# Decoder layer on one core: attention scores with the keys stationary and the queries moving

## The reference, cut to what matters

```
x = x + rg_lru(layernorm(x))
ln = layernorm(layernorm(x)); xn = layernorm(ctx)
q = (ln @ Wq + bq) * 128**-0.5
k, v = split(concat([xn, ln], axis=1) @ Wkv + bkv)
out = softmax(q k^T) v                       # per batch and head: 100 x 822
x = x + (out merged over heads) @ Wo + bo
x = x + expert(argmax(route)) * max_prob     # per token
```

## Time and profile before

| | us |
|---|---|
| three runs of the kernel | 1041.38, 1042.39, 1042.47 |
| median of the runs | 1042.39 |
| span of the profiled execution, first to last instruction | 1041.8 |
| recurrent block and projections, up to the first score | 160.6 |
| the eight batches, first score to first product with Wv | 527.2 |
| Wv, Wo, router, experts | 354.0 |

### The profile page before, as it was taken

How to read it: one execution, slowest core, us unless ns; L and a number is a source line. 1 busy time by engine, 2 the same in 40 slices (tenths; PEclk the granted TensorE clock), 3 DMA queues, 4 the chain that set the end, 5 groups by cost and what they waited for, 6 DMA issues and landing times.

```text
span 1041.8 us, 18196 instructions
## 1 busy us (share of the span) xinstructions
PE 1019.0 (98%) x6086; PEld 934.4 (90%) x6087; DVE 811.0 (78%) x1392; ACT 561.8 (54%) x1111; POOL 115.4 (11%) x98
## 2 busy tenths in 40 slices
PE   8999999999999999999999999999999999999997
PEld 7969998999999999999999999998967788888886
DVE  7888666888979879798797996675858856947992
ACT  4425575445544455454554545573646756847871
POOL 3623200000000000000000000000011111211221
PEclk9999999999999999999999999999999999999999
DMA  8433884343323443234433335479367974956970
GB/s 273 128 116 128 308 300 164 91 172 121 112 93 96 170 119 109 98 96 154 131 95 116 96 93 178 145 253 323 108 189 258 340 259 154 358 184 223 363 270 22
DMA packets 110279, 182.47 MB, mean 175 GB/s; under 512 B 32464, under 2 KB 53456, under 8 KB 108322
## 3 DMA queue, kind: packets, MB, share of 16 engines
q1 hardware_dynamic: 108562, 177.45, 50.8%
q0 software_dynamic: 1680, 4.54, 1.3%
HBM read 145.84 MB, written 37.11 MB: 176 GB/s over the span
## 4 chain that ended last, share of the span: by engine, by line
PE 83%; DVE 7%; issue 3%; DMA 3%; ACT 2%; SPq 1%; ACTq 0%; POOL 0%; DVEq 0%; POOLq 0%
PE bank L641 24%; PE bank L643 24%; PE bank L642 24%; PE bank L1177 4%; PE bank L1316 1%; PE bank L1195 1%; PE bank L1164 1%; PE bank L1162 1%; PE bank L1194 1%; DMA w<-in_WoT 1%; DMA stage<-in_W 1%; DVE hs L1716 1%; SPq L686 1%; DVE xn_l L1645 1%; DMA scr_q<-st 1%
## 5 line engine op out<-in xcount | busy, mean ns | idle before, releaser
L641 PE MATMUL bank<-pt_h,xn_h 128*128 128x256 f32 (+1 forms) x576 | 167.4, 291 | 0.0
L643 PE MATMUL bank<-pt_h,xn_l 128*128 128x256 f32 (+1 forms) x576 | 164.8, 286 | 0.0
L642 PE MATMUL bank<-pt_l,xn_h 128*128 128x256 f32 (+1 forms) x576 | 164.7, 286 | 0.0
L1645 DVE TENSOR_TENSOR wsl<-stage,wsh 128x2048 fp32r<-128x2048 f32 x63 | 143.8, 2292 | 24.6 <-ACT wsh L1496 19.8
L641 PE MATMUL bank<-xt_h,qt_h 128*128 128x410 f32 (+1 forms) x384 | 136.4, 355 | 1.2 <-ACT pr L1451 1.2
L642 PE MATMUL bank<-xt_l,qt_h 128*128 128x410 f32 (+1 forms) x384 | 134.1, 349 | 0.0
L643 PE MATMUL bank<-xt_h,qt_l 128*128 128x410 f32 (+1 forms) x384 | 134.1, 349 | 0.0
L1496 ACT CAST wsh<-stage 128x2048 fp32r<-128x2048 f32 x63 | 120.5, 1920 | 12.6 <-PE bank L643 8.0
L641 PEld LDWEIGHTS bank<-pt_h,xn_h 128*128 128x128 f32 x576 | 109.0, 189 | 1.3 <-issue 0.2
L642 PEld LDWEIGHTS bank<-pt_l,xn_h 128*128 128x128 f32 x576 | 109.1, 189 | 0.0
L643 PEld LDWEIGHTS bank<-pt_h,xn_l 128*128 128x128 f32 x576 | 109.0, 189 | 0.0
(11 more groups left out here) (266 smaller groups left out, 2418.0 us busy)
## 6 DMA issues: line engine op xcount, KB each, us to landing
stage<-in_W SPq DMA_DIRECT2D x63, 1024.0 KB, 6.1
scr_q<-st SPq DMA_DIRECT2D x16, 800.0 KB, 4.2
qf<-scr_q SPq DMA_DIRECT2D x8, 1600.0 KB, 6.6
zr<-scr_z SPq DMA_DIRECT2D x16, 800.0 KB, 5.5
scr_z<-zf SPq DMA_DIRECT2D x7, 1600.0 KB, 5.2
rt<-in_ctxT SPq DMA_DIRECT2D x7, 1444.0 KB, 12.9
raw<-in_ctx SPq DMA_DIRECT2D x8, 768.0 KB, 4.6
mrow<-scr_rows SPq DMA_DIRECT2D x14, 361.0 KB, 3.9
```

The lines of the kernel that those rows point to most:

```text
L641: pe.matmul(dest, lh, rh, start=start and k == 0, stop=False)
L642: pe.matmul(dest, lh, rl, start=False, stop=False)
L643: last = pe.matmul(dest, ll, rh, start=False, stop=stop and k == n - 1)
L1645: return dve.tensor_tensor(dst, src, high.bitcast(F32), ALU.subtract)
```

## The change

The scores are computed transposed. A batch is two units of four heads (400 queries), unit u = 2b or 2b + 1. For a unit, 7 chunks of keys are stationary and the 400 query columns move; so are the context products (rows stationary, 400 weights moving), and no weights are transposed any more. ScalarE copies each score bank to `pa`, scaled by the inverse deviation of the context row, which is a factor per partition now. The maximum over keys runs over chunks on VectorE (`maximum`), then over partitions: TensorE transposes the 128 x 400 maxima (`turn_maxima`), VectorE reduces them and builds a diagonal (`shifts`), TensorE spreads them by a product with ones (`spread_maxima`). VectorE adds them to the scores (`shift`), ScalarE exponentiates in place and makes the high part with the same scale (`exponentials`, `weights_high`), VectorE the low part (`weights_low`). The sums over keys are added on VectorE (`add_up`), summed over partitions and spread by a product with ones (`spread_sums`); their reciprocal is taken over the whole 128 x 400 bank (`inverse`), and VectorE multiplies the results of the context products with it as it copies them out of their bank (`weighted`), where ScalarE then adds beta. The context rows need one pass instead of two on VectorE, the keys too. The plan and its loops are gone: the order is written out per engine. The rows of the next batches have a second buffer (`raws[1]`), which lies over `wv_h` and `wv`.

TensorE:

```diff
-                            if k < RT - 1:
-                                last = split_products(
-                                    pe, s_pair[k % 2][half][:, 0:SH[half]],
-                                    [((qt_h[:, c, k * P:(k + 1) * P], qt_l[:, c, k * P:(k + 1) * P]),
-                                      (xt_h[:, c, cols], xt_l[:, c, cols])) for c in range(ND)], True, True)
...
-                                last = pe.transpose(t[:, n * P:n * P + r], pr[k % 3][0:r, c * P:(c + 1) * P],
-                                                    ident[0:r, 0:r])
...
+            def scores(u, c):
+                b, g = divmod(u, 2)
...
+                dest, cols = score_bank(u, c)[:, 0:GR], group_cols(u)
+                if c < MC:
+                    keys = slice(c * P, (c + 1) * P)
+                    last = split_products(pe, dest, [((xt_h[:, d, keys], xt_l[:, d, keys]), (qt_h[:, d, cols], qt_l[:, d, cols]))
+                                                     for d in range(ND)], True, True)
+                else:
+                    for d in range(ND):
+                        both = xt_h[:, d, KLOW:KLOW + 2 * DUP]
+                        pe.matmul(dest, both, qt_h[:, d, cols], start=d == 0, stop=False)
+                        last = pe.matmul(dest, both, qt_l[:, d, cols], start=False, stop=d == ND - 1)
+                last.then_inc(s_s, 1)
...
+            def turn_maxima(u):
+                pe.wait_ge(s_mx, u + 1)
...
+                for j in range(GH):
+                    last = pe.transpose(mbank[0:T, j * P:(j + 1) * P], mx[:, j * T:(j + 1) * T], ident[:])
+                last.then_inc(s_mt, 1)
...
+            def spread_maxima(u):
+                pe.wait_ge(s_dg, u + 1)
...
+                pe.matmul(nbank[:, 0:GR], ones[0:T, :], dg[0:T, :], start=True, stop=True).then_inc(s_spread, 1)
...
+            def spread_sums(u):
+                pe.wait_ge(s_sum, u + 1)
...
+                pe.matmul(mbank[:, 0:GR], ones[:], sm[:], start=True, stop=True).then_inc(s_spread, 1)
...
+            def context(u, dc, between=lambda: None):
+                b, g = divmod(u, 2)
+                n = ND * u + dc
+                if n >= 2:
+                    pe.wait_ge(s_zn, n - 1)
...
+                for c in range(KC):
+                    if dc == 0:
+                        pe.wait_ge(s_p, KC * u + c + 1)
...
+                    if c == KC // 2:
+                        between()
...
+            for u in range(1, NU):
+                for c in range(KC):
+                    scores(u, c)
+                    if u == 1 and c == 0:
+                        turn_maxima(0)
+                    elif u == 1 and c == 2:
+                        spread_maxima(0)
+                    elif u > 1 and c == 3:
+                        spread_sums(u - 1)
+                if u == 1:
+                    context(0, 0)
+                    spread_sums(0)
+                    context(0, 1)
+                    turn_maxima(1)
+                    context(0, 2)
+                    spread_maxima(1)
+                    context(0, 3)
+                else:
+                    context(u - 1, 0, lambda: turn_maxima(u))
+                    context(u - 1, 1, lambda: spread_maxima(u))
+                    context(u - 1, 2)
+                    context(u - 1, 3)
```

SyncE, where the second attention stage begins and where it ends:

```diff
+            sp.wait_ge(s_rawz, 2)
+            load_rows_raw(1)
+            load_keys(1)
...
-            sp.wait_ge(s_ktl, B * ND)
-            sp.dma_start(wv[:], a["Wv"].rearrange("(c p) n -> p c n", p=P)).then_inc(s_wvd, 16)
...
+            sp.wait_ge(s_xnl, 3 * B)
+            sp.dma_start(wv[:], a["Wv"].rearrange("(c p) n -> p c n", p=P)).then_inc(s_wvd, 16)
```

VectorE, its new functions and the places in its order that the prediction speaks of (`u` runs over the units, `g` is 1 for an odd one):

```diff
+            def maximum(u, c):
...
+                ch.add(dve.tensor_tensor(mx[0:n, :], mx[0:n, :], pa[k][0:n, c, :], ALU.max))
...
+            def shift(u, part):
...
+                dve.tensor_tensor(at, at, nbank[0:n, 0:GR].unsqueeze(1).broadcast_to([n, len(cs), GR]), ALU.add).then_inc(s_sub, 1)
...
+            def inverse(u):
+                dve.wait_ge(s_spread, 2 * u + 2)
...
+                dve.reciprocal(inv[:], mbank[:, 0:GR]).then_inc(s_inv, 1)
...
+            rows_stats(1, 0)
+            maximum(0, 1)
+            rows_stats(1, 1)
+            for c in range(2, 5):
+                maximum(0, c)
+            rows_norm(1, 0)
+            rows_norm(1, 1)
+            maximum(0, 5)
+            maximum(0, MC)
...
+                if g and b + 1 < B:
+                    keys_transposed(b + 1, 0)
+                elif g:
+                    values_low(0)
+                    values_low(1)
+                elif b + 1 < B:
+                    rows_stats(b + 1, 1)
+                shifts(u)
+                if g and b + 1 < B:
+                    keys_transposed(b + 1, 1)
+                elif g == 0 and b + 1 < B:
+                    queries(b + 1, 0)
+                weighted(u - 1, 0)
+                shift(u, 0)
+                shift(u, 1)
+                shift(u, 2)
```

More of the change, by code:

```diff
@@ L408, in build @@
     ohi = mem("ohi", [P, NT, NSLOT], F32R)
-    assert mem.at <= mem.where(zf)
-    s_x = [sem(f"s_xin{b}") for b in range(B)]
+    assert mem.at <= tail_at
+    s_x = [sem(f"s_xin{g}") for g in range(3)]
     s_w3 = [sem(f"s_w3_{k}") for k in range(3)]
@@ L971, in router_std @@
                 pool.sem_inc(s_rsx, 1)
-            def run(b, events):
-                for what, k in events:
-                    if what == "B" and k == 1:
-                        rows_std(b)
-            run(0, rest)
-            batches(pool, lambda b, events: steps(run, b, events), ch, POOL_B)
+            for b in range(1, B):
+                rows_std(b)
             for b in range(NT):
@@ L1904, in finish @@
                         else:
[L1905 removed]
+                            for g in range(2):
+                                dve.wait_ge(s_zd[g], 16 * B)
                         r = tile_rows(b)
@@ L1986, in _ @@
-            tally(s_padp)
-            run(0, rest)
-            batches(dve, batch, ch, DVE_B)
+            dve.memset(xn_h[DUP:P, MC, :].bitcast(F32), 0.0)
+            for k in range(2):
+                dve.memset(pl[k][DUP:P, MC, :].bitcast(F32), 0.0)
+                dve.wait_ge(s_ltout[k], 32 * B // 2)
+            rows_stats(1, 0)
[5 more added lines that the diff above has]
+            rows_norm(1, 1)
@@ L1990, in _ @@
+            weighted(NU - 2, ND - 1)
+            values_low(2)
+            values_low(3)
+            inverse(NU - 1)
+            weighted(NU - 1, 0)
+            low_unit(0)
+            low_unit(1)
+            weighted(NU - 1, 1)
+            low_unit(2)
+            output_low(0)
+            output_low(1)
+            weighted(NU - 1, 2)
+            low_unit(3)
+            output_low(2)
+            output_low(3)
+            weighted(NU - 1, 3)
             finish(tail)
```

1094 lines of the change are left out of this document (595 added, 499 removed), and 6 rows, old and new, of the table plan.

## The result

| | before | after |
|---|---|---|
| median of 4 runs, us | 1042.42 | 1110.11 (1109.71 to 1111.37) |
| ratio to before, 95% interval | | 1.0653 (1.064 to 1.0667) |
| span of the profiled execution | 1041.8 | 1108.0 |
| up to the first score | 160.6 | 175.4 |
| first score to first product with Wv | 527.2 | 575.9 |

The account below looks back on a forecast made before the run. TensorE paces the old kernel, VectorE's queue the changed one: 160.6 + 66.0 + 6 x 67.7 + 31.5 + 60.1 = 724.4, + 354.0 + 3 = 1081.4, with 0.6 more 1082 us; range 1041 to 1094.

Parts of the forecast that it names:

- TensorE would gain 28 us in all: TensorE's own work in attention: a batch falls to 62.3 us, 3.5 less per batch, 28 in all.
- the split one (0.18): Rival for the products with ones: 0.18 us each, reciprocal cheap too; batch 62.0, total 1036; chance 0.10.
- The reciprocal, 3.5: VectorE's reciprocal of the sums, once per unit: 3.5 us, about the middle between 0.57 and 7.0.
- the forecast's own case: Reciprocal between 2.5 and 4.5 us, total 1066 to 1094; chance 0.60.
- The high end: Rival: the reciprocal repeats 17 ns per element, 7.0 us; 74 and more per batch, total over 1120; dearer reciprocal's chance 0.08.
- A steady batch, 67.7: Two steady units, even 32.6 and odd 35.0 us, TensorE waiting for VectorE's maxima; 1.9 more than today.
- VectorE sets the pace: Steady units: VectorE needs 29.3 us plus the reciprocal against TensorE's 31.15; any reciprocal over 1.9 makes VectorE the bound.
- The end, 8 us behind `wv`: Last unit: TensorE waits 8 us for `spread_maxima(15)`, as Wv's late load and parts stand ahead of `shifts(15)`.
- The beginning, 66.0: First score to `scores(2, 0)`: 66.0 us, including TensorE's waits for VectorE's queue.
- where PE's own work is 47: The beginning up to `scores(2, 0)`: TensorE's own work is 47 us of the 66.0.
- Everything before 160.6 and behind is otherwise taken as equal: Head before the first score stays 160.6 us; the part from Wv on stays 354.0, apart from 3 more.
- The range: Total time 1041 to 1094 us, leaving out cheap products with ones and the dearer reciprocal.

Follow-up runs that it names:

- r6: Changed kernel with the reciprocal placed behind the last row remainders on VectorE in odd units; 1120.38 us, ratio 1.0737.
- r13: r6 with 18 products of idle data on TensorE ahead of `turn_maxima` in odd units; 1108.78 us, ratio 1.0625.
- r1: Changed kernel with the reciprocal replaced by a multiplication with a constant, leaving out the normalisation; 1109.73 us, ratio 1.0641, a batch 64.3.
- r10: Changed kernel with the inverse of the sums made on ScalarE as logarithm and exponential, not on VectorE; 1091.65 us, ratio 1.048.
- r7: Changed kernel with a key pass, half the statistics and work ahead of the shift moved later in VectorE's queue; 1116.5 us, ratio 1.0684.
- r14: r12 with the even units' first weighted result ahead of the queries and Wv's parts in the last unit's gaps; 1056.41 us, ratio 1.0132.
- r12: r8's head, a reordered beginning, r4, r9 and r10 combined, plus later turning of maxima and further queue moves; 1059.21 us, ratio 1.0154.
- r9: Changed kernel with VectorE adding up the last unit's sums before the previous unit's last weighted result; 1103.91 us, ratio 1.0597.
- r4: Changed kernel with the high and low parts of Wv behind the last unit's weights on both engines; 1107.19 us, ratio 1.0614.
- r5: Changed kernel with TensorE's five waits in the first two units filled with idle products; 1107.74 us, ratio 1.0602.
- r2: Changed kernel with latent keys respaced in the head's projections and SyncE's stores of them moved alike; 1104.57 us, ratio 1.059.
- r8: r2 with each latent key block stored as one piece of 1600 bytes per partition; 1099.23 us, ratio 1.051.

## Why the prediction was right and wrong

- **TensorE would gain 28 us in all: about 20.** A batch has 63.05 us of busy TensorE where the sum had 62.3 and the kernel before has 65.59, so 2.5 per batch and not 3.5. The products with ones cost 0.67, nearer to the plain price (0.82) than to the split one (0.18). The transposes are gone as read from the earlier trace rows.
- **The reciprocal, 3.5: over-priced.** It is 2.64 (2.55 after overlap, for 3.4), between the ends 0.57 and 7.0 and inside the forecast's own case. The high end fails since the 17 ns more of one element do not repeat per element: (2.64 - 0.15) / 400 is 6.2 ns.
- **A steady batch, 67.7: measured 67.5, by two errors that cancel.** With the measured reciprocal the same working gives 66.0. It also lacked the wait of 2.1 us in the odd units for the last row remainders: it let TensorE start the context products of an even unit as soon as the scores were done, but in the order of VectorE the remainders stand behind the reciprocal. That wait is not the 1.5 us between 66.0 and 67.5, though. r6 removes it, and the turn waits as much longer; with the clock held up (r13) the batch is 67.7. What is left is the length of VectorE's queue: the turn stands 18.5 and 21.2 us behind the first score of its unit (457.01 and 489.61 in the trace), where the working with the measured reciprocal has 17.95 and 20.45. That is 1.3 of the 1.5; which terms of the queue were too small was not taken apart. So the reciprocal was priced 1.7 a batch too high and the rest 1.5 too low, and that 67.7 met 67.5 is luck.
- **VectorE sets the pace: right**, shown by r1 and r10 (3 us per batch), and by r6, r7 and r14, where the wait moved when its place was changed, and r12, where most of it did (0.7 us came off a batch). But it is not full (62.8 of 67.5): r9 shows that 1 us of a batch was a loop in which VectorE waits for TensorE too.
- **The end, 8 us behind `wv`: right**, 7.19. r4 takes it away; nearly half comes back in the products with Wv.
- **The beginning, 66.0: 12.9 short, and this step failed.** Waits were forecast at 19 and were 21.6. The first was 9.67 and not 4.4, because the second half of the rows of batch 1 landed 16.4 after the first score, where the sum took 4.6 us from their issue; that they share the queue with `rt`, queries and latent keys may be the reason, but no run tried it. The larger error is the clock: "where PE's own work is 47" priced all products at 0.181, and behind four of the five waits they came at 0.333: 57.3 us for the 47. The profile before could have warned: its distance rests on a TensorE that is busy 98%, at clock 1.00. r5 and r13 show that the clock stays up when the waits are filled, and r5 that 6 of the 10 us were lost through it.
- **"Everything before 160.6 and behind is otherwise taken as equal": wrong by 14.8 us in the head, the largest single error, and this step failed too.** No wait of the trace before could have shown it. The diff did: `latent_keys`, two buffers laid over `mx` and `sm`, a wait of VectorE on a store, and the stores on SyncE's queue behind waits of its own. r2 and r8 show two parts of it, 6.3 us the order of the buffers and of their stores, and 3.3 the form of the stores; 5.2 stay open. With the beginning it makes 27.7, a little more than the 26.6 by which the sum was short.
- **The range** was made from the unknown price of an operation. What it lacked was a case for the places of the program that were not looked at.

## What to carry to other kernels

When a change touches a list of orders, go through *every* function that the diff adds or calls, the head's too, and ask of each wait which queue stands behind it; a stretch is equal only where the diff leaves its queues alone. When a forecast contains waits of TensorE, price the work behind them at the lower clock as a second case, also where the waits are short. And a gain in a stage that one engine paces is worth what leaves that engine's queue; rearranging the queue mostly moves the wait, as in r6, r7 and r14, and for the greater part in r12.

## What the runs showed of the hardware that was not expected

- **A wait of TensorE can cost more than its length.** Behind waits of 2.87, 3.77, 3.85 and 9.67 us, and one of 3.16 that follows another of 2.10, products of 400 columns came every 0.333 us, which is the 1.2 GHz level, for another 3 to 6 us, and then every 0.181 again. Eighteen useless products in the wait made a kernel of 1120.4 us run in 1108.8 (r6 and r13). The Trainium skill, "TensorE: Matmul & The Clock Gate" (Part 1: The HAM clock gate), says that the clock granted to the array is set by how busy TensorE has been recently; the trace agrees, and these runs give the price in a kernel that is busy 92%.
- **Short waits bring the clock down in some batches and not in others.** Behind waits of 2.0 to 2.1 us it fell for 3.4 us in two of six steady batches of the changed kernel, at no cost; behind 1.9 us it fell in four of six of r7, and these take 68.7 to 68.8 us for the 67.2 and 67.5 of the others. The length of a wait alone did not tell which.
- **A reciprocal of 128 x 400 float32 on VectorE is 2.64 us, 4.6 times an ordinary operation of that size**; on ScalarE, as logarithm and exponential, it is 3.6 us of which 2.56 are table loads, and cheaper here, because ScalarE had 30 us per batch to spare (busy 36.7 of 67.5).
- **Short pieces seem to fill the DMA engines.** In 30 us of the head in which latent keys are stored in pieces of 400 and 40 bytes, 16 engines were busy 1.00 at 272 GB/s; with pieces of 1600 bytes, in half as many stores, 0.87 at 302 GB/s (r2 and r8).
